# Pacing indirect row fetches: waits by half batch ahead of a mixing block's rounds, and a fetch distance of four instead of eight in expert loops

## What is computed

```python
# layer 0
h = layernorm(x) * (1 + ca) + sa
x = x + ga * selective_scan_block(h)           # conv, scan over 16 states
h = layernorm(x) * (1 + cb) + sb
x = x + gb * top2_of_8_experts(h)              # silu(h Wg) * (h Wu) Wd, weighted
# layer 1
h = layernorm(x) * (1 + ca) + sa
x = x + ga * layernorm(h + chunked_ssd(h) W_out)   # conv, silu, decays by head
h = layernorm(x) * (1 + cb) + sb
x = x + gb * top1_of_8_experts(h)              # relu(h W1 + b1) W2 + b2
```

## Time and profile before

| | |
|---|---|
| median of 3 runs | 1211.58 us (1209.12 to 1213.8) |
| the profiled execution's own time | 1211.7 us |
| its span | 1209.9 us |
| busy share of the span: PE, DVE, POOL, ACT | 73%, 73%, 60%, 52% |
| expert loop of layer 0, from POOL's first fetch to the last turn | 550 to 674 us |
| middle block, from POOL's first fetch | from 683 us |
| expert loop of layer 1 | 1071 to 1155 us |
| fetches of the expert loops, x112 | 125.8 us busy on POOL |
| fetches of the middle block, x64 | 62.7 us busy on POOL |

### The profile page before, as it was taken

The page is one execution under the profiler, slowest core; times in us unless marked ns, Lnnn a source line. Parts: engine busy times, 40 slices in busy tenths (PEclk is TensorE's granted clock), DMA queues, the critical chain, the costliest instruction groups (busy, mean ns, idle before and its releaser), DMA issues. The chain is left out here.

```text
span 1209.9 us, 14980 instructions
## 1 busy us (share of the span) xinstructions
PE 888.1 (73%) x4244; PEld 572.2 (47%) x4244; DVE 886.0 (73%) x1790; ACT 630.6 (52%) x1401; POOL 731.5 (60%) x508
## 2 busy tenths in 40 slices
PE   8888779869986868735999432697988978339930
PEld 4333334334433423335999411365655667239930
DVE  4897999799989999783766532786896778554522
ACT  4787546764776464352443200756567584236620
POOL 0898799898989999304666374155432443047546
PEclk8899979988988988856999765898988887569975
DMA  6645345445444545131333211111102020242223
GB/s 182 184 120 144 122 150 176 129 142 166 156 142 140 168 151 176 49 144 33 86 86 77 56 52 33 53 32 49 44 3 60 27 72 18 71 147 69 64 61 96
DMA packets 90905, 118.95 MB, mean 98 GB/s; under 512 B 12508, under 2 KB 48804, under 8 KB 90696
## 3 DMA queue, kind: packets, MB, share of 16 engines
q1 hardware_dynamic: 84168, 104.34, 28.0%
q0 software_dynamic: 6656, 13.64, 4.7%
HBM read 103.70 MB, written 14.25 MB: 97 GB/s over the span
## 5 line engine op out<-in xcount | busy, mean ns | idle before, releaser
L687 POOL TENSOR_TENSOR ma_bu<-ma_u,ma_row_b 128x1024 f32<-128x1024 f32 x128 | 298.6, 2356 | 16.0 <-DVE ma_u L898 8.0
L416 PE MATMUL y_ps<-ma_h,ident 128*128 128x512 f32 x512 | 259.7, 647 | 25.6 <-POOL ma_h L697 21.5
L1215 POOL DMA_INDIRECT s_rows<-xs,take x112 | 125.8, 1123 | 163.9 <-POOLq L951 105.5
L563 ACT ACTIVATE decay_ps<-ma_delta,negA 128x512 f32<-128x512 f32 x256 | 172.5, 686 | 84.4 <-DVE ma_h L790 81.5
L416 PEld LDWEIGHTS y_ps<-ma_h,ident 128*128 128x128 f32 x512 | 102.3, 208 | 156.9 <-issue 116.3
L1568 POOL TENSOR_TENSOR mi_dec<-mi_dec,mi_gm 128x512 f32<-128x512 f32 x32 | 40.7, 1271 | 163.1 <-DVE mi_gm L2024 108.5
L1232 PE MATMUL s_up_ps<-s_xt,s_w 128*128 128x128 f32 x896 | 126.0, 287 | 10.4 <-ACT s_xt L1259 5.6
L1232 PEld LDWEIGHTS s_up_ps<-s_xt,s_w 128*128 128x128 f32 x896 | 116.4, 203 | 10.9 <-issue 10.8
L780 DVE TENSOR_TENSOR_SCAN decay_ps<-decay_ps,ma_carry,ma_bu 128x512 f32<-128x512 f32 x88 | 110.2, 1273 | 10.9 <-issue 8.0
L790 DVE TENSOR_TENSOR ma_h<-decay_ps,ma_row_c 128x512 f32<-128x512 f32 x176 | 117.7, 669 | 0.0
L697 POOL TENSOR_TENSOR ma_h<-ma_h,ma_row_c 128x1024 f32<-128x1024 f32 x40 | 97.0, 2425 | 16.5 <-DVE ma_h L780 14.6
(11 more groups left out here) (323 smaller groups left out, 1778.3 us busy)
## 6 DMA issues: line engine op xcount, KB each, us to landing
ma_row_b<-bc_rows SPq DMA_DIRECT2D x128, 256.0 KB, 3.6
ma_row_c<-bc_rows SPq DMA_DIRECT2D x128, 256.0 KB, 3.4
mi_cs<-cs_rows SPq DMA_DIRECT2D x32, 256.0 KB
ys<-s_outs SPq DMA_DIRECT2D x28, 256.0 KB
w<-in_experts SPq DMA_DIRECT2D x1, 4112.0 KB, 14.8
w<-in_experts SPq DMA_DIRECT2D x1, 3072.0 KB, 10.3
xs<-rows SPq DMA_DIRECT2D x4, 512.0 KB, 3.4
out<-X SPq DMA_DIRECT2D x8, 256.0 KB
```

Of the source, the lines that this page charges most:

```text
L416: mm = pe.matmul(y_ps[:, j, :], m.ident[:], h[g % HS][:, j, :], start=False, stop=True, skip_group_check=True)
L563: act.activation(decay[s % DS][:], delta[b % 2][:, j, col(c)], ACT.Exp, scale=m.negA0[:, j, n:n + 1]).then_inc(decay_done, 1)
L687: pool.tensor_tensor(bu[g % BUS][:], u[b % 2][:, :, col(c)], both(row_b[g % BS]), ALU.mult).then_inc(bu_done, 1)
L1215: pool.indirect_dma_start(rows[s % ROWS][:], None, m.xs[layer], bass.IndirectOffsetOnAxis(ap=m.take[:, s:s + 1], axis=0)).then_inc(fetched ...
```

## The change

Two things in the order of POOL's fetches; nothing is computed differently, and no other engine's list changes.

In the expert loops the fetch of slot `s` waits for the turn of slot `s - 4` instead of `s - 8`. There are still eight buffers.

In the middle block the 48 fetches ahead of the rounds keep their order. Four waits come between the groups of eight: ahead of batch 1's first half for the first four normalized tiles of batch 0, ahead of its second half for all eight, ahead of batch 2's first half for ACT's read of the last raw piece of batch 0's second half, ahead of its second half for `exps(0)`.

```diff
--- before.py
+++ after.py
@@ -1186,7 +1186,7 @@
     UP = 2 * F0 if layer == 0 else F1
     width = WIDTH[layer]
     GROUP, READ = 4, 8
-    ROWS, WS, HS = 8, 7, 3
+    ROWS, AHEAD, WS, HS = 8, 4, 7, 3
     tag = f"s{layer}_"
     with ExitStack() as ctx:
         sb = lambda name, shape, dt=F32: ctx.enter_context(nc.sbuf_tensor(tag + name, shape, dt))
@@ -1210,8 +1210,8 @@
         def _(pool):
             pool.wait_ge(m.rows_stored, 16 * NBATCH * (layer + 1))
             for s in range(slots):
-                if s >= ROWS:
-                    pool.wait_ge(turned, base + s - ROWS + 1)
+                if s >= AHEAD:
+                    pool.wait_ge(turned, base + s - AHEAD + 1)
                 pool.indirect_dma_start(rows[s % ROWS][:], None, m.xs[layer], bass.IndirectOffsetOnAxis(
                     ap=m.take[:, s:s + 1], axis=0)).then_inc(fetched[s % ROWS], 16)
 
@@ -1568,8 +1568,17 @@
                 pool.tensor_tensor(mixing, mixing, four(gm[T % 2][:]), ALU.mult).then_inc(m_done, 1)
 
             for n in range(3):
-                for i in range(2 * GROUP * GROUPS):
-                    gather(n, i)
+                for g in range(GROUPS):
+                    if (n, g) == (1, 0):
+                        pool.wait_ge(n10_xn, GROUP)
+                    elif (n, g) == (1, 1):
+                        pool.wait_ge(n10_xn, BT)
+                    elif (n, g) == (2, 0):
+                        pool.wait_ge(piece_read, read("raw", 0, 3, 1))
+                    elif (n, g) == (2, 1):
+                        pool.wait_ge(exps_done, 1)
+                    for i in range(g * 2 * GROUP, (g + 1) * 2 * GROUP):
+                        gather(n, i)
 
             for b in ROUNDS:
                 sent = 0
```

## The result

| | median | lowest to highest | runs |
|---|---|---|---|
| kernel before | 1212.41 us | 1209.12 to 1213.8 | 4 |
| changed kernel | 1180.36 us | 1176.89 to 1182.46 | 4 |

The ratio is 0.9741, 95% interval 0.9715 to 0.9767: 32 us or 2.6% faster. The forecast was 1190 us with a range of 1166 to 1211. The profiled execution of the changed kernel took 1176.9 us with a span of 1175.1, 34.8 less than the span before; it is the shortest of the four runs.

The account below looks back on a forecast made before the run. The prediction took stops of PE, ACT and DVE beside POOL's back to back gathers as the loss; 18.0 us (middle block) + 3.6 (expert loops) = 21.6 off 1211.7 gave 1190.0 us, range 1166 to 1211.

Parts of the forecast that it names:

- The bound and the stop: Middle block's start and expert loops' starts: engines read late, without work behind it, beside POOL's back to back gathers.
- The weak point named: At both places: that stops go with back to back gathers beside a working PE is a reading, not in the trace.
- (a): Middle block, wait ahead of batch 1, half 0: gives nothing; first 24 gathers run as before and the stop begins again.
- (b): Middle block, wait ahead of batch 1, half 1: stop ends at 715.5, PE's transposes come at 718.3 instead of 742.16.
- The zero: Middle block: PE's transposes of the second half, from which later times are counted; forecast at 718.3.
- (c): Middle block, remaining 24 gathers: a second stop of 12.3 us after 8 or 9 gathers; `mix` at 760.8, 18.0 us gained.
- (d): Expert loops' threshold: POOL's burst ends earlier, eight gathers unchanged; 3.6 us gained, bounds 0 and 14.9.
- (e): Moved middle block gathers, if all as long as the loops' longest, 1.505 us: 7.8 us of gain lost; taken as nothing.
- The sum: Whole kernel: 18.0 + 3.6 = 21.6 us off 1211.7, giving a median of 1190.0.
- the stops go altogether: Rival, middle block and expert loops: pauses keep whatever fills up from filling; 47.0 us gained, 1165; chance 0.17.
- the slower one: Rival, middle block: each of three later bursts stops ACT for its length plus a tail; 18.9 us later, 1230.5; chance 0.08.

Follow-up runs that it names:

- the wide fill: Kernel before, plus a 128 x 512 POOL fill, counting up and awaiting a semaphore, behind each of the 48 prologue gathers: 1189.72 us, ratio 0.9837.
- the half rows: Kernel before, with the 32 prologue gathers of batches 1 and 2 fetching 64 of their 128 rows: 1204.43 us beside 1206.83.
- the second session: Changed kernel run again beside the kernel before, both unaltered, stops present: 1182.3 us against 1212.79, ratio 0.9746.
- the first session: Threshold alone, waits alone, small fill on the kernel before, and change with threshold 3: ratios 1.001, 0.9996, 1.002, 1.0045; kernel before 1155.37 us, no stops.
- the best version: Changed kernel with POOL's pauses moved and the last eight prologue gathers put behind the first mix products: 1167.8 us, ratio 0.9654; again 1164.9 us, 0.9635.

## Why the prediction was right, and where not

**The bound and the stop.** That the prologue and the loops' starts lose time in which no engine works, and that this goes with back to back gathers, was right; the wide fill and the half rows show it. The weak point named, that the trace can't say what the stop is, is narrower now: the issuing of indirect DMAs on POOL, one per 1.25 us, in a state of the machine that isn't always there. My reading that it needs a working PE was not tested; once there, a stop goes on without one, as PE did nothing from 713.91 to 742.16 in the kernel before.

**(a)** Right: the first wait was met. The first 24 gathers ran unbroken and the first stop set in.

**(b)** Right in mechanism and size. I let the stop end 2.3 us behind POOL's last gather (705.82) and it ended 2.7 behind it (708.54; 3.5 in the second session). The zero was forecast at 35.5 us behind the first gather and came at 36.2.

**(c)** The result is right, 79.5 us of prologue against 78.0 forecast, and the second stop cost 79.5 - 36.2 - 30.2 = 13.1 us against 12.3. Its course was not as worked out. It set in after 15 gathers from the restart, not 8 or 9; ACT was past `exps` by then (726.8), so the wait ahead of the last eight gathers was met and POOL never paused there. The stop ended its first hole while POOL was still issuing, and went on in smaller ones. That the size agrees is therefore partly luck, the more so as some 3 of the 13.1 us are PE's lower clock behind the hole, which my sum didn't have; in the second session the same sum gives 15.1 us. Three of the four waits held nothing in this execution: the first was met, as in (a), the raw piece had been read at 721.4, just before POOL came to its gather, and `exps` were done at 726.8. The whole gain of the middle block is that of one wait, the one that held POOL 5.88 us.

**(d)** This is the step that failed: "I take 3.6 since the onset comes at about the ninth gather, ahead of what moves." It gave 6.2 + 6.1 = 12.3 us, close to the upper bound of 14.9. That the first eight gathers would be unchanged was right, and a short delay at the old place was there. My mistake was to take the stop's length as settled at its onset. The ninth gather moved by 1.5 us instead of the 0.3 of my sum, since POOL itself saw turn 4 late (done at 559.65, the gather at 560.82), and behind that pause turn 6 came 2.2 us after turn 5. I read this as: the pause ended the stop before it had grown. No run moves the ninth gather alone, and by (c) a hole can also end while POOL is still issuing, so what sets a stop's length stays open.

**(e)** Gathers were longer in places (up to 1.42 us in the prologue) and it cost nothing, since POOL had 12 us to spare ahead of `mix`. It did cost in the first session: there one gather took 3.99 us, beside DVE's convolutions, and POOL came last. So the 1.505 us that I took for the longest was too short, and the bound of 7.8 us was not tested by the run of the whole change. The Trainium skill ("SBUF — State Buffer", section "SBUF: two separate sides") states that GpSimd can't write the descriptors of a DMA while VectorE runs an fp32 copy from SBUF to SBUF in its two-port mode. The trace agrees in direction: in the loop of layer 1, where each of DVE's copies of 1156 columns takes 0.75 us, the median gather took 1.43 us, against 0.95 in layer 0, where DVE copies 768. But this depends on the threshold: in the first session the medians of layers 1 and 0 were 1.13 and 1.10 us with threshold 8, and 1.43 and 0.95 with 4. So the change moves gathers against the copies; the loop of layer 1 took 85.3 to 85.4 us all the same.

**The sum.** 18.0 + 3.6 = 21.6 us forecast; 16.4 + 12.3 = 28.7 measured in the two parts, of 32 between the medians. So the middle block's term was 1.6 us too large and the loops' 8.7 too small; of the 10 us by which 1190 misses the median, 7 are in these two terms and 3 in stretches that the change doesn't touch. The rival "the stops go altogether" was nearly true for the loops and not for the middle block; the slower one had no trace for it, as no burst cost more than it saved. A rival was missing: that the gain might hang on a state of the machine. In the first session the change's two parts gave nothing, 1.001 and 0.9996.

## What to carry to other kernels

When all engines stand still together beside a queue that keeps issuing, look at the issuing engine's rhythm, not only at who waits for whom: here 24 of 48 prefetches could be issued later, at 4.3 us of the prologue and nothing measurable of the whole where nothing stopped, and the best version kept bursts beside other work to 12 and left the last eight for the gaps of the next phase (no run shows that 12 is a limit). For this kernel a prefetch was best as far ahead as its use needs and no further; distance that nobody needed cost what no count of bytes or of busy engines shows. And compare in more than one session before a gain of this kind is believed or given up: the same kernel took 1155 us in one and 1206 to 1213 in four others.

## What the runs showed of the hardware that I had not expected

- Beside indirect DMAs that POOL issued 1.20 to 1.26 us apart, ACT, DVE and POOL itself came late out of their waits, by up to 21 us at a time, with the DMA engines 20% busy (11% with half the rows). At 1.66 us apart, with a fill and its wait between them, there were no such holes. Halving the rows of each changed little (prologue 94.4 us in place of 95.9).
- The steady loop of layer 0 (a gather per slot) is slower in the sessions with stops: 58 turns from 575.7 to 666.8 us in the changed kernel, 1.59 us each; in the session without stops 62 turns from 571.0 to 659.6, 1.45 each. It is not the clock, granted at 1.00 in both; ACT's longest wait for a product of PE is 1.7 us in the one and 0.6 in the other, so I take it for short delays of the same kind. Some 9 us of that loop are lost there with threshold 4 or 3 alike (125 to 126 us for the loop; without stops 115.7 with threshold 4 and 118.9 with 3), and the kernel before is no better (1.57 us a turn):

```profile
L1224 PE MATMUL s_xt_ps<-ident,s_rows x58: 272/273/273, 575.7 to 666.8; 128*128 128x128 f32 x58
...
L1224 PE MATMUL s_xt_ps<-ident,s_rows x62: 272/273/273, 571.0 to 659.6; 128*128 128x128 f32 x62
```

- The state comes and goes by session. It was there in four of five, on four chips, and on one chip once there and once not; the first comparison had it too. Inside a session all runs of a kernel agree within 0.7% (26 runs of the kernel before in the one without). What sets it stays open: I found nothing in the profiles that tells the two apart but the late waits themselves. Whether it takes a working PE, and what POOL's issuing shares with the other engines' waits, wasn't tried.
